# The order of the first mix and the turn of the next keys on TensorE, in a fused attention kernel on one core

## The reference, cut to what matters

```python
qkv = shift_token(x) @ wqkv
q = l2norm(q) * qs; k = l2norm(k) * ksc
q, k = rotary_xpos(q, k)
# local attention: a window of 128 queries sees its own and the previous 128 keys
sim  = einsum('bhwid,bhwjd->bhwij', bq, bk)          # masked
attn = softmax(sim)
o    = einsum('bhwij,bhwjd->bhwid', attn, bv)
x = x + o @ wo
h = layernorm(shift_token(x)) @ w1 + b1               # two halves a, g
x = x + (a * gelu(g)) @ w2 + b2
```

## Time and profile before

| what | value |
|---|---|
| median of three runs | 2846.29 us |
| the profiled execution, its own time | 2850.04 us |
| its span in the trace | 2848.2 us |
| PE busy in the span | 2650.9 us (93%) |
| DVE busy | 2229.4 us (78%) |
| ACT busy | 1517.7 us (53%) |
| POOL busy | 1459.2 us (51%) |
| chain that ended last, by engine | PE 39%, DVE 4%, issue 3%, POOL 2%, ACT 1% |

### The profile page before, as it was taken

The page is one execution under the profiler, slowest core; times in us unless marked ns, Lnnn a source line. Parts: engine busy times, 40 slices in busy tenths (PEclk is TensorE's granted clock), DMA queues, the critical chain, the costliest instruction groups (busy, mean ns, idle before and its releaser), DMA issues.

```text
span 2848.2 us, 61433 instructions
## 1 busy us (share of the span) xinstructions
PE 2650.9 (93%) x21416; PEld 2154.0 (76%) x21416; DVE 2229.4 (78%) x5244; ACT 1517.7 (53%) x3106; POOL 1459.2 (51%) x1408
## 2 busy tenths in 40 slices
PE   6799999999999999999738899999989999999987
PEld 4577788777888778878636688888878778888875
DVE  7688868776777787788757888888878888888874
ACT  3444454445445534544116667667756666676651
POOL 2343444344334444454436766665656666677643
PEclk9999999999999999999968999999999999999998
DMA  3100000010000010000021000000100100000001
GB/s 98 27 9 9 16 1 16 16 29 1 2 1 16 9 36 16 16 23 16 30 72 31 17 16 13 16 16 13 31 28 21 40 15 30 28 31 28 31 15 39
DMA packets 77715, 65.63 MB, mean 23 GB/s; under 512 B 15378, under 2 KB 72682, under 8 KB 77418
## 3 DMA queue, kind: packets, MB, share of 16 engines
q1 hardware_dynamic: 77418, 61.70, 7.3%
HBM read 49.10 MB, written 12.58 MB: 22 GB/s over the span
## 4 chain that ended last, share of the span: by engine, by line
PE 39%; DVE 4%; issue 3%; POOL 2%; ACT 1%; SPq 1%; DMA 0%; POOLq 0%; DVEq 0%; ACTq 0%
PE PS L263 31%; PE PS L708 3%; PE PS L664 1%; PE PS L673 1%; PE PS L738 1%; DVE PS L1473 1%; DVE SQ L1455 0%; POOL VL L1705 0%; DVE PT L1489 0%; DVE VH L1201 0%; PE PS L764 0%; ACT PR L1065 0%; PE PS L626 0%; DVE KQ L1462 0%; DVE ZS L1588 0%
## 5 line engine op out<-in xcount | busy, mean ns | idle before, releaser
L1065 ACT ACTIVATE PR<-PS,SM 128x256 f32<-128x256 f32 (+1 forms) x512 | 279.4, 555 | 95.4 <-DVE SM L1478 93.6
L917 ACT ACTIVATE FB<-PS,BC 128x512 f32<-128x512 f32 x192 | 132.3, 689 | 322.7 <-PE PS L263 322.1
L1731 POOL TENSOR_TENSOR RL<-FB,RH 128x512 fp32r<-128x512 f32 x96 | 123.7, 1288 | 289.9 <-DVE RH L1239 289.9
L1261 DVE TENSOR_TENSOR U<-PS,CST 128x512 f32<-128x512 f32 x384 | 236.3, 677 | 24.7 <-PE PS L263 24.7
L263 PE MATMUL PS<-XTH,WH 128*128 128x512 f32 x576 | 241.7, 420 | 12.7 <-ACT FB L917 5.8
L1473 DVE CUSTOM_DVE_ANT_0 PS<-PS,MSK 128x256 f32<-128x256 f32 (+1 forms) x512 | 202.7, 436 | 44.3 <-PE PS L263 42.8
L263 PE MATMUL PS<-WH,RH 128*128 128x256 f32 x768 | 223.2, 291 | 14.2 <-POOL RL L1731 7.3
L1239 DVE CAST RH<-FB 128x512 fp32r<-128x512 f32 x192 | 83.8, 437 | 186.2 <-ACT FB L917 186.2
L263 PE MATMUL PS<-XTL,WH 128*128 128x512 f32 x576 | 227.5, 395 | 0.0
L263 PE MATMUL PS<-XTH,WL 128*128 128x512 f32 x576 | 227.2, 394 | 0.0
L925 ACT COPY NUM<-PS 128x256 f32<-128x256 f32 x96 | 35.8, 373 | 354.6 <-DVE TMP L1253 303.6
(11 more groups left out here) (213 smaller groups left out, 8815.3 us busy)
## 6 DMA issues: line engine op xcount, KB each, us to landing
PX<-in_L_attn_x SPq DMA_DIRECT2D x16, 512.0 KB, 4.0
TB<-in_k_rot SPq DMA_DIRECT2D x64, 128.0 KB, 2.1
SG<-in_L_attn_W SPq DMA_DIRECT2D x24, 256.0 KB, 2.7
xp_scratch<-PX SPq DMA_DIRECT2D x8, 512.0 KB, 2.9
xs_scratch<-X SPq DMA_DIRECT2D x64, 64.0 KB, 1.5
ZS<-xs_scratch SPq DMA_DIRECT2D x16, 256.0 KB, 2.8
GG<-xp_scratch SPq DMA_DIRECT2D x8, 512.0 KB, 3.8
out<-GG SPq DMA_DIRECT2D x8, 512.0 KB, 3.8
```

Source lines behind the costliest of these rows:

```text
L917: e.activation(FB[:, hb % 2, :], PS[:, 5, :], ACT.Relu, bias=BC[:, l % 2, 4 + hb:5 + hb]).then_inc(*a_re.up(n, hb))
L1065: t = e.activation(PR[:, par, 256 * i + lo:256 * i + hi], PS[:, 3 + par, 256 * i + lo:256 * i + hi], ACT.Exp, bias=S[:, 40 + 2 * g + i:41 ...
L1261: e.tensor_tensor(heads(U[:, u % 6, :], 4), heads(PS[:, g, :], 4), bcast(CM, 4), ALU.mult).then_inc(*d_mk.up(n, u))
L1731: e.tensor_tensor(RL[:, r, :], FB[:, 0, :], RH[:, r, :].bitcast(F), ALU.subtract).then_inc(*p_rl.up(n, hb))
```

## The change

`mix(u, 0)` moves up, from behind the MLP piece to directly behind `scores(u, 1)`. The turn of the next keys and, in kinds 1 to 3, the MLP piece come behind it. No instruction is added or taken away, and no wait is changed; only TensorE's list has another order.

```diff
@@ -845,6 +845,7 @@
             else:
                 fall(q, 4)
             scores(u, 1)
+            mix(u, 0)
             turn_k(u + 1)
             if i == 1:
                 partner(q, 2)
@@ -852,7 +853,6 @@
                 fall(q, 2)
             elif i == 3:
                 fall(q, 5)
-            mix(u, 0)
             if i == 0:
                 partner(q, 0)
             turn_q(u + 1)
```

## The result

The changed kernel takes **2863.7 us** (median; 2853.85 to 2865.62), the kernel before, run beside it, 2846.66 us (2845.73 to 2848.42). The ratio is 1.0051 with a 95% interval of 1.0041 to 1.0061: slower by 12 to 17 us. The forecast was +7.7 us and 2854.0, with a range up to 2860, so the time lies above the range. The sign is right; the forecast size is about half of what came.

The account below looks back on a forecast made before the run. PE's pace bounds bodies 8 to 29, waits between engines count in 0 to 7. Gains in kinds 0 to 3 against losses in layer 2's kind 3, bodies 0 to 7, 62 and 63 sum to +7.7: 2854.0 us, range 2848 to 2860.

Parts of the forecast that it names:

- The move on PE: PE's list in every body: one visit less to the full array shape, 0.15 us off in kinds 1 to 3, 0.20 in kind 0.
- the two ends for the passage from scores to mix: PE's new passage, taken as 1.06 us: 0.1 less without a gap, 0.1 more if two shape changes count twice; 6 us either way.
- Kinds 0 and 1: 14 bodies each: later exponentials leave 0.07 us gain a body in kind 0, 0.03 in kind 1; sums -1.0 and -0.4.
- The expected wait: Kind 0, turn of weights on PE: a wait of some 0.13 us with the hand-over, for ACT's later exponentials.
- a sign of being wrong: The forecast would be wrong if, among other signs, kinds 0 and 1 grow.
- The rival of the close calls: Kinds 0 to 2: DVE's copy or exponentials 0.15 us later, 39 bodies lose 0.15, +5.9, total +13.6, 2859.9 us; chance 0.13.
- Bodies 0 to 7: Bodies without MLP: later copies of keys and queries cost 0.9 us in five bodies, 0.15 in three; sum +4.95.
- Kind 3 in layer 2: Bodies 43, 47, 51, 55, 59: fall, `add_y` and norm operations beside `finish` end 1.02 us later, second mix waits; +5.1.
- "slower still" case: Rival in kinds 0 to 2: copy or exponentials 0.15 us later in 39 bodies, +5.9, total +13.6, 2859.9 us; chance 0.13.
- Body 62: No `ask_k` or `ask_q` any more, but loses like the bodies without MLP: +1.0 us.
- Bodies 38 to 40: Near 0 in all; in body 38 DVE is behind with weight splits, +0.2 us.

## Why the prediction was right in sign and short in size

- **The move on PE**: right. 0.15 less in each body of kinds 2 and 3 was forecast, and 17.74 to 17.57 and 17.78 to 17.63 came. Of the two ends for the passage from scores to mix, neither held; it is 1.06.
- **Kinds 0 and 1**: near for kind 0 in the mean (-0.05 a body for -0.07), but five of the eight bodies stay within 0.01 us. The expected wait is there: in body 24 of the changed kernel the turns of weights start 0.38 us behind the last matmul (1961.02 to 1961.40), 0.23 in the earlier trace rows. Kind 1 grew, 23.24 became 23.27 to 23.29, where -0.03 was forecast; the prediction had named that as a sign of being wrong, here of 0.04 us a body. The rival of the close calls, 0.15 for each of 39 bodies, did not come: kinds 0 to 2 together are -1.5 us.
- **Bodies 0 to 7**: the term of +4.95 is near what they cost with as much half clock (5.8 to 6.1 by three traces, 3.9 us by the medians of the run with this part alone). The changed kernel's own profile has +0.80. In body 5, `ask_k` waits 0.24 us for ACT's copy of the keys, and the second mix comes 1599.83 - 1591.01 = 8.82 us behind the second scores, where it was 1601.34 - 1593.40 = 7.94: +0.88, forecast 0.9.

```profile
1591.01 1.13 PE L263 MATMUL PS<-KT,QT 64*128 64x256 f32 x8 [1.06 <-DVE PT L1489]
1594.43 0.50 PE L263 MATMUL PS<-VH,XBH 128*128 128x512 f32 x1 [0.24 <-ACT KT L1044]
1599.83 0.73 PE L263 MATMUL PS<-PT,VV 128*64 128x128 f32 x9 [0.62 <-DVE PT L1489]
```

- **Kind 3 in layer 2: the step that failed.** "the mix waits 1.02 + 0.15 more than before, and nothing gained on PE counts. Sum 5 x 1.02 = +5.1." Cause, place and length of the wait are right, to 0.01 us. Its price is not: in the changed kernel each time that PE is idle for 2.89 us, work at 1.2 GHz follows. Five of these bodies and the ones behind them cost +15.73 us in place of the forecast's +4.75; with the idleness filled they cost +5.0. The prediction priced a wait as its length alone, and took for granted that PE goes on at the clock it had before; for the waits of 1.73 us in these bodies that had been so. No rival had it either: the "slower still" case came to +13.6 with 5.9 us put on other places, kinds 0 to 2.
- **Body 62**: +1.20 (forecast +1.0).
- **Bodies 38 to 40**: +1.65 (forecast near 0). Their length goes by the stretches of half clock in them, in all twelve traces: 64.31 us with none (the old order in kind 3 of layer 2), 65.54 to 65.73 with one (the kernel before is here), 67.20 to 67.32 with two (the changed kernel). Each stretch begins 0.3 to 1.2 us behind a wait of TensorE ahead of `out_proj`. The trace of the kernel before has this already; two such waits, and the windows behind them:

```profile
2247.94 0.36 PE L263 MATMUL PS<-VH,OTH 128*128 128x256 f32 x1 [1.75 <-issue]
2290.48 0.36 PE L263 MATMUL PS<-VH,OTH 128*128 128x256 f32 x1 [2.25 <-issue]
```

```profile
2248.90:2252.30 3.40, 3.40 (x16) 3.30 (x16) 3.15 (x6) 2.31 (x7) 2.77 (x4) 0.50 0.12 26
2290.50:2294.00 3.50, 3.50 (x25) 3.19 (x26) 3.50 (x7) 1.58 (x6) 3.50 (x3) 1.00 0.06 19
```

The shorter wait has a fall behind it and the longer one has none. Over the twelve traces the clock fell behind 11 of 24 such waits of 1.75 us and behind 5 of 12 of some 2.2 us. So no length of a wait, by itself, divides the ones that keep the clock from the ones that lose it.

Split by medians, an estimate over runs on different chips: the changed kernel costs 17.0 us. With the old order in layer 2's kind 3 2.1 is left, so these bodies, 63 among them, hold 14.9. The spare turns take away 17.0 - (2856.89 - 2849.08) = 9.2 of it, which is about the clock's part; 5.7 are left to the waits, for which the forecast had 5.1 + 0.7. The traces give 10.7 for the clock and 5.0 for the waits of the five bodies. Bodies 0 to 7 don't add up in this way: alone they cost 3.9, more than the 2.1 of the 58 bodies that they are among.

**Left open**: why the clock falls behind some waits of 1.75 to 2.88 us and not behind others of the same length; and why the changed kernel's times run from 2853.85 to 2869.73 us over all its executions when both profiled ones show the same five falls.

## What to carry to other kernels

Where TensorE's wait grows, price not only its length but what the clock does behind it: look in the trace for waits of TensorE with a fall behind them, short ones too, and give a fall a chance and a price of its own (here some 2.1 us beside a wait of 2.9). That the clock stays whole behind a wait at one length says nothing of a longer one at the same place. A reordering that gains a tenth of a microsecond a body on TensorE can be lost many times over in the few bodies where the step that is pushed back starts the chain that PE will wait for. There, the chain is the thing to shorten (two operations moved behind the copy brought 0.32%), and if a wait with a fall behind it can't be shortened, filling it with spare turns can be cheaper than leaving it empty (9.2 us here, by medians).

## What the runs showed of the hardware that was not expected

- In kind 3 of layer 2 the granted clock fell to 1.2 GHz in 16 of 20 cases with 2.84 to 2.89 us of idle TensorE (ten of ten, four of five, two of five), with 1.73 us in none of fifteen. In bodies 38 to 40 it fell behind 11 of 24 waits of 1.75 us. In body 51 a fall nearly doubled the mix (1.09 to 1.98 us) and the next scores (1.13 to 2.08). It cost 10.7 us over five waits, some 2.1 each, beyond the wait itself.
- 24 turns of a constant in such a wait kept the clock at 1.00, in five of five.
- Four norm operations take 1.67 us alone and 4.94 to 5.33 beside GpSimd's `finish`. The Trainium skill (SBUF — State Buffer, Who interferes with whom) says that DVE and GpSimd share a pair of ports which one of them holds at a time; the trace agrees with a slowdown, 1.67 / 4 = 0.42 us for one of them alone and 1.24 to 1.33 beside `finish`; no run here shows the ports themselves.
- Scores to mix, a change of shape on both sides of the array, takes 1.06 us, as any other step behind scores: one gap, not two.
